# Transposes grouped by PSUM bank, one copy per group, in three places of an attention and feed-forward kernel

## What is computed

```python
def _L0_attn_ref(x, w_qkv, w_out):
    qkv = (x @ w_qkv).reshape(b, s, 3, HEADS, HEAD_DIM)
    q, k, v = (qkv[:, :, 0], qkv[:, :, 1], qkv[:, :, 2])
    scores = jnp.einsum('bqhd,bkhd->bhqk', q / sqrt(HEAD_DIM), k)
    scores = jnp.where(causal_mask[None, None], scores, NEG)
    attn = jax.nn.softmax(scores, axis=-1)
    return jnp.einsum('bhqk,bkhd->bqhd', attn, v).reshape(b, s, HIDDEN) @ w_out

def _L0_ffn_ref(x, weight, lora_A, lora_B, router_w):
    base = jnp.einsum('btd,od->bto', x, weight)
    probs = softmax(jnp.einsum('btd,ed->bte', x, router_w))
    # w_dense: the two largest, normalised, zeros elsewhere
    Ax = jnp.einsum('nd,erd->ner', x_flat, lora_A)
    expert_out = jnp.einsum('ner,ne,eor->no', Ax, w_dense, lora_B) * SCALING
    return base + expert_out.reshape(B, T, OUT_F)

x = x + _layernorm(_L0_attn_ref(_layernorm(x), w_qkv, w_out))
x = x + _layernorm(_L0_ffn_ref(_layernorm(x), weight, lora_A, lora_B, router_w))
```

## Time and profile before

| | us |
|---|---|
| median of 3 runs | 2517.46 (2517.17 to 2564.19) |
| the profiled execution | 2518.34 |
| its span on the slowest core (core 2) | 2516.8 |
| spans of the eight cores | 2499.6 to 2516.8 |

### The profile page before, as it was taken

The page is one execution under the profiler, slowest core; times in us unless marked ns, Lnnn a source line. Parts: engine busy times, 40 slices in busy tenths (PEclk is TensorE's granted clock), DMA queues, the critical chain, the costliest instruction groups (busy, mean ns, idle before and its releaser), DMA issues.

```text
span 2516.8 us, 28407 instructions; the slowest of 8 cores (2499.6 to 2516.8 us)
## 1 busy us (share of the span) xinstructions
PE 1788.2 (71%) x9387; PEld 928.9 (37%) x9552; DVE 742.5 (30%) x2497; ACT 691.8 (27%) x1393; POOL 42.1 (2%) x59
## 2 busy tenths in 40 slices
PE   1228878887887887788789788459990555666654
PEld 1114444444444444344444444224440233233332
DVE  4552122122212212221221222114442244333342
ACT  2221242143133214313322431302121233333331
POOL 0000000000000000000000000000000000000000
PEclk9998878977887897888788789679995777777777
DMA  7212011011101101110110100351218200000000
GB/s 151 101 67 26 1 26 26 4 23 26 26 1 26 26 1 26 26 25 2 26 26 1 26 1 1 55 112 67 84 67 141 43 34 34 17 34 34 34 34 34
DMA packets 48653, 95.25 MB, mean 38 GB/s; under 512 B 5248, under 2 KB 38144, under 8 KB 42368
## 3 DMA queue, kind: packets, MB, share of 16 engines
q0 software_dynamic: 46064, 76.58, 15.7%
q1 hardware_dynamic: 2448, 16.85, 2.0%
HBM read 119.67 MB, written 16.78 MB: 54 GB/s over the span
## 4 chain that ended last, share of the span: by engine, by line
PE 65%; ACT 12%; DVE 9%; issue 8%; another core or an unknown queue 4%; DVEq 0%; DMA 0%; ACTq 0%; POOL 0%; SPq 0%; POOLq 0%
PE P_qkv L303 26%; PE P_b L680 10%; PE P_qkv L453 9%; ACT expT L399 7%; PE P_e L534 4%; PE P_o L534 4%; DVE sst L151 3%; PE P_t L341 2%; ACT expT L425 2%; PE P_u L636 1%; PE P_qkv L416 1%; DVE Vaug L349 1%; ACT xln L250 1%; PE P_x L667 1%
## 5 line engine op out<-in xcount | busy, mean ns | idle before, releaser
L303 PE MATMUL P_qkv<-A,wbf 128*128 128x512 bf16 x3008 | 661.4, 380 | 20.6 <-DVE att L470 17.2
L303 PEld LDWEIGHTS P_qkv<-A,wbf 128*128 128x128 bf16 x3072 | 300.0, 98 | 377.0 <-issue 19.5
L453 PE MATMUL P_qkv<-Vaug,expT 128*128 128x129 bf16 x2176 | 258.4, 304 | 18.8 <-DVE srcp L464 15.7
L680 PE MATMUL P_b<-A,x2T 128*128 128x512 bf16 x992 | 241.3, 405 | 4.4 <-issue 3.5
L453 PEld LDWEIGHTS P_qkv<-Vaug,expT 128*128 128x128 bf16 x2176 | 223.7, 141 | 35.8 <-issue 27.6
L425 ACT ACTIVATE expT<-P_sc,cbuf 128x512 bf16<-128x512 f32 (+1 forms) x128 | 74.8, 585 | 544.3 <-PE P_t L341 542.0
L636 PE MATMUL P_u<-cbuf,xln 128*128 128x128 bf16 x256 | 54.8, 260 | 199.7 <-ACT x2T L643 180.0
L326 DVE CAST Kbf<-P_qkv 128x512 bf16<-128x512 f32 x64 | 44.3, 692 | 419.1 <-PE P_qkv L303 419.1
L680 PEld LDWEIGHTS P_b<-A,x2T 128*128 128x128 bf16 x1024 | 106.4, 105 | 135.6 <-issue 33.0
L534 PE MATMUL P_e<-wo_bf,A 128*128 128x512 bf16 x501 | 112.9, 383 | 56.2 <-DMA wo_bf<-w_out 55.6
L435 DVE TENSOR_TENSOR expT<-expT,cbuf 128x128 bf16<-128x128 bf16 x256 | 57.5, 225 | 321.4 <-ACT expT L425 314.7
(11 more groups left out here) (82 smaller groups left out, 1613.7 us busy)
## 6 DMA issues: line engine op xcount, KB each, us to landing
wbf<-wqkv POOLq DMA_DIRECT2D x16, 1536.0 KB, 14.3
expT<-x SPq DMA_DIRECT2D x16, 1024.0 KB, 6.0
xio<-x POOLq DMA_DIRECT2D x16, 1024.0 KB, 5.1
out<-ost POOLq DMA_DIRECT2D x16, 1024.0 KB, 4.6
wo_bf<-w_out POOLq DMA_DIRECT2D x2, 4096.0 KB, 41.5
A<-weightT POOLq DMA_DIRECT2D x2, 4096.0 KB, 42.2
sat<-at POOLq DMA_DIRECT2D x1, 512.0 KB, 57.2
sbf<-bflat POOLq DMA_DIRECT2D x1, 512.0 KB, 60.0
```

What stands on the lines that cost most here:

```text
L303: _q=col0, _p=wpar: e.matmul(P_qkv[:, _q:_q + 512], wbf[:, 6144 * _p + 384 * _c + 128 * _m: 6144 * _p + 384 * _c + 128 * _m + 128], A1[:, ...
L453: _q=qt: e.matmul(P_qkv[:, _a:_a + 129], expT[:, 512 * _i + 128 * _u: 512 * _i + 128 * _u + 128], Vaug[:, 129 * _i:129 * _i + 129], start= ...
L680: e.matmul(P_b[:, 512 * _f:512 * _f + 512], x2T[:, 2048 * _p + 128 * _c: 2048 * _p + 128 * _c + 128], A2[:, 2048 * _c + 512 * _f: 2048 * _ ...
```

## The change

In all three places, transposes are grouped: several go into one PSUM bank side by side, only the last one signals, and one copy with a strided access pattern takes them all. The data, the number of transposes and the banks used are the same.

- Layer norm 1: 4 groups of 4 transposes; 4 copies of 512 columns in place of 16 of 128 (destination: four runs of 128 columns, 2048 apart).
- V: 2 groups of 8; 2 copies of 1024 columns in place of 16 (destination: eight runs of 128 at a pitch of 129). The first transpose of a group waits for two blocks of VTs in place of one.
- Feed-forward: 2 groups of 8; 2 ScalarE copies of 1024 columns in place of 16; `x2T_ready` of a chunk is now its group's copy.

```diff
-                for ch in range(NCH):
-                    slot = ln1_slots[(16 * t + ch) % 8]
-                    bank = (16 * t + ch) % 8
...
+                for grp in range(4):
+                    bank = (4 * t + grp) % 8
+                    slot = ln1_slots[bank]
+                    gwb = B.gw([bank])
+                    for j in range(4):
+                        ch = 4 * grp + j
+                        B.emit("tensor", lambda e, _p=par, _c=ch, _j=j,
+                               _pt=slot: e.transpose(
+                                   _pt[:, 128 * _j:128 * _j + 128],
+                                   xln[:, 2048 * _p + 128 * _c:
+                                       2048 * _p + 128 * _c + 128], sid),
+                               waits=([(c["act"], xlv), consts_c] + gwb)
+                               if j == 0 else (),
+                               inc=(c["pe"] if j == 3 else None))
+                    tv = c["pe"].v
+                    dv = B.emit("vector", lambda e, _t=t, _g=grp, _pt=slot:
                                 e.tensor_copy(
+                                    A1[:].rearrange("p (c f) -> p c f",
+                                                    f=2048)
+                                    [:, 4 * _g:4 * _g + 4,
+                                     128 * _t:128 * _t + 128],
+                                    _pt[:, 0:512].rearrange(
+                                        "p (c f) -> p c f", f=128)),
                                 waits=[(c["pe"], tv)], inc=c["dve"])
...
-                for k in range(NCH):
-                    pt = P_t1 if k % 2 == 0 else P_t2
-                    bank = 6 + k % 2
...
+                for grp in range(2):
+                    pt = P_t1 if grp == 0 else P_t2
+                    bank = 6 + grp
+                    gwb = B.gw([bank])
+                    for j in range(8):
+                        k = 8 * grp + j
...
+                               waits=([(c["dve"],
+                                        max(vt_block[2 * grp],
+                                            vt_block[2 * grp + 1]))] + gwb
...
+                               if j == 0 else (),
+                               inc=(c["pe"] if j == 7 else None))
+                    tv = c["pe"].v
+                    av = B.emit("vector", lambda e, _g=grp, _pt=pt:
                                 e.tensor_copy(
+                                    Vaug[:].rearrange("p (k f) -> p k f",
+                                                      f=129)
+                                    [:, 8 * _g:8 * _g + 8, 0:128],
+                                    _pt[:, 0:1024].rearrange(
+                                        "p (k f) -> p k f", f=128)),
+                                waits=[(c["pe"], tv)], inc=c["dve"])
...
-                for ch in range(NCH):
-                    pt = P_u1 if ch % 2 == 0 else P_u2
-                    bank = 6 + ch % 2
...
+                for grp in range(2):
+                    pt = P_u1 if grp == 0 else P_u2
+                    bank = 6 + grp
+                    gwb = B.gw([bank])
+                    for j in range(8):
+                        ch = 8 * grp + j
...
+                               waits=([(c["act"], xl2)] + gwb) if j == 0
+                               else (), inc=(c["pe"] if j == 7 else None))
+                    tv = c["pe"].v
+                    av = B.emit("scalar", lambda e, _p=par, _g=grp, _pt=pt:
                                 e.activation(
+                                    x2T[:, 2048 * _p + 1024 * _g:
+                                        2048 * _p + 1024 * _g + 1024],
+                                    _pt[:, 0:1024], AF.Copy),
                                 waits=[(c["pe"], tv)], inc=c["act"])
                     B.sg([bank], c["act"], av)
-                    x2T_ready[ch] = av
+                    for j in range(8):
+                        x2T_ready[8 * grp + j] = av
```

More of the change, by code:

```diff
@@ L336, in build_program @@
                 vt_dve = c["dve"].v
-                for k in range(NCH):
-                    pt = P_t1 if k % 2 == 0 else P_t2
-                    bank = 6 + k % 2
[L341 to L348, removed]
-                                e.tensor_copy(
-                                    Vaug[:, 129 * _k:129 * _k + 128],
-                                    _pt[:, 0:128]), waits=wv, inc=c["dve"])
+                for grp in range(2):
[4 more added lines that the diff above has]
+                        k = 8 * grp + j
+                        B.emit("tensor", lambda e, _k=k, _j=j, _pt=pt:
+                               e.transpose(
+                                   _pt[:, 128 * _j:128 * _j + 128],
+                                   VTs[:, 128 * _k:128 * _k + 128], sid),
+                               waits=([(c["dve"],
+                                        max(vt_block[2 * grp],
+                                            vt_block[2 * grp + 1]))] + gwb
+                                      + ([(c["dve"], vaug_ones)]
+                                         if h == 0 and grp == 0 else []))
+                               if j == 0 else (),
+                               inc=(c["pe"] if j == 7 else None))
+                    tv = c["pe"].v
+                    av = B.emit("vector", lambda e, _g=grp, _pt=pt:
+                                e.tensor_copy(
+                                    Vaug[:].rearrange("p (k f) -> p k f",
[4 more added lines that the diff above has]
+                                waits=[(c["pe"], tv)], inc=c["dve"])
@@ L631, in build_program @@
                 xl2 = xl2_next
-                for ch in range(NCH):
-                    pt = P_u1 if ch % 2 == 0 else P_u2
-                    bank = 6 + ch % 2
[L635 to L642, removed]
+                for grp in range(2):
[4 more added lines that the diff above has]
+                        ch = 8 * grp + j
+                        B.emit("tensor", lambda e, _p=par, _c=ch, _j=j,
+                               _pt=pt: e.transpose(
+                                   _pt[:, 128 * _j:128 * _j + 128],
+                                   xln2[:, 2048 * _p + 128 * _c:
+                                       2048 * _p + 128 * _c + 128], sid),
+                               waits=([(c["act"], xl2)] + gwb) if j == 0
+                               else (), inc=(c["pe"] if j == 7 else None))
+                    tv = c["pe"].v
+                    av = B.emit("scalar", lambda e, _p=par, _g=grp, _pt=pt:
                                 e.activation(
-                                    x2T[:, 2048 * _p + 128 * _c:
-                                        2048 * _p + 128 * _c + 128],
-                                    _pt[:, 0:128], AF.Copy),
+                                    x2T[:, 2048 * _p + 1024 * _g:
+                                        2048 * _p + 1024 * _g + 1024],
+                                    _pt[:, 0:1024], AF.Copy),
                                 waits=[(c["pe"], tv)], inc=c["act"])
                     B.sg([bank], c["act"], av)
-                    x2T_ready[ch] = av
+                    for j in range(8):
+                        x2T_ready[8 * grp + j] = av
                 B.sg([("xln2", par)], c["pe"], c["pe"].v)
```

11 lines of the change are left out of this document (removed).

## The result

The changed kernel takes 2367.45 us (median; the kernel before, on the same chip, 2517.55), a ratio of 0.9393 with the interval 0.9378 to 0.9408: faster by 6.1%. The profiled execution took 2361.73 us, its span 2360.2 us, and 156.6 us less than the profiled execution before. Some executions of these kernels, in which the cores of a die run at a lower clock, take some per cent longer; they count in the medians given here, not in the ratios, intervals and profiles.

What follows compares the result with a forecast made beforehand. Only the heads were taken as near TensorE's limit; transpose-copy alternations lay on the chain of heads and feed-forward tiles. 2518.3 less 56 (V), 60 (x2T) and 2 (layer norm 1), clock at nothing, gave 2400 us, range 2370 to 2440.

Steps and rivals of the forecast that it cites:

- V's transposes: In each head, grouped transposes and two merged copies save 3.5 us; sixteen heads: 56 us (45 to 62).
- The spacing: Between V's grouped transposes in a head: taken as 0.09 us, with bounds 0.06 and 0.13.
- Rival 1: Strided copies run one element at a time (V: 1.21 us each); 2423 us in all; chance 0.12.
- x2T: In the feed-forward, two ScalarE copies of 1.02 us let P_b start 4.0 us sooner a tile; fifteen tiles: 60 us.
- wait for su: Feed-forward: su is ready with 5 us of room; its transpose waiting for ScalarE would prove the forecast wrong.
- Layer norm 1: Its grouped transposes and copies save 0.1 us a tile; 16 tiles: 2 us (5 gained to 4 lost).
- Clock: Granted clock's effect set to nothing; bounds 1 us either way a head, 1.3 gained to 1.7 lost a feed-forward tile.
- the middle stages: Output projection and two weight loads, between heads and feed-forward: not touched, forecast saving 0.
- Rival 3: Clock gives: V done before 768.8, first scores fast, P_b warms sooner; 36 us more, 2365 to 2385; chance 0.08.
- Rivals 2: Clock takes back 26 us in P_b and 16 in heads: 2442, up to 2467; chance 0.09, another 0.04 within 2%.
- 4: Feed-forward: P_b never gets full clock, 27.3 us a tile's 64 matmuls; 195 us lost, 2595 us in all; chance 0.02.
- 5: A hidden wait (bank guard, drains of att) holds the second group: within 2%, counted in a chance of 0.04.

Runs made afterwards that it cites:

- pad19: The changed kernel with one VectorE memset of 1024 columns behind V's copies in each head, holding up the scores; 2357.3 us in one profiled execution.
- pad37: The changed kernel with two VectorE memsets (4096 and 192 columns) behind V's copies in each head, holding up the scores; 2428.4 us, ratio 0.9635.
- ffn_only: The kernel before with only the feed-forward's x2T transposes grouped; 2452.0 us, ratio 0.9779.
- v_only: The kernel before with only V's transposes grouped; 2437.1 us, ratio 0.9664.
- ffn_early: The changed kernel with the next tile's x2T transposes and copies planned ahead of this tile's layer norm 3; 2302.8 us, ratio 0.915.
- best: ffn_early plus vwait, with the next tile's layer norm 2 moved behind the router and su in the queues; 2214.6 us, ratio 0.8788.
- small: The changed kernel with V and x2T transposes still grouped, but sixteen copies of 128 columns back to back; 2387.2 us, ratio 0.9483.
- pad11: The changed kernel with one VectorE memset of 64 columns behind V's copies in each head; 2384.0 us in one profiled execution.
- vwait: The changed kernel with score matmuls waiting for V's last cast instead of the last copy into Vaug; 2328.4 us, ratio 0.9247.

## Why the prediction was off

**V's transposes: right.** 3.5 us a head forecast, 3.7 measured (59 us for 56). The spacing was taken as 0.09 us and was (0.61 - 0.22) / 7 = 0.056, the other bound. The merged copy cost 0.689 us for 0.69. Rival 1, one element at a time (1.21 us), is refuted. The Trainium skill's page "VectorE: DVE Perf Modes", section "Mode 2×_1P — pack two bf16 into one 32-bit read", asks for a 4-byte aligned start; half of this copy's eight runs begin on 2-byte addresses, and all 32 copies took 683 to 696 ns. The measurement decides against that rule for this case.

**x2T: right.** From the tile's layer norm 3 statistics to its P_b it was 15.39 us before (2088.00 to 2103.39) and is 11.36 after (1984.44 to 1995.80): 4.03 us for 4.0, 60.5 us in all. The copies took 1.014 us for 1.02, so bf16 and f32 do lie on one line on ScalarE. TensorE did not wait for su.

**Layer norm 1: at the good end of its bounds.** In its timeline the sixteen transposes now stand in 1.86 us, (1.86 - 0.31) / 15 = 0.103 us apart:

```profile
104.94 1.86 PE L263 MATMUL P_qkv<-cbuf,xln 128*128 128x128 bf16 x16 [8.85 <-ACT xln L250]
105.64 1.71 DVE L272 COPY A<-P_qkv 128x512 bf16<-128x512 bf16 x4 [3.19 <-PE P_qkv L263]
107.26 2.46 DVE L151 BATCH_NORM_STATS2 sst<-expT 128x6 f32<-128x512 f32 x4
```

The forecast had named 0.107 for transposes without a semaphore each, 0.2 us a tile, and took 0.1, 2 us in all, with 5 us as the bound. The tile period is 10.82 us for 11.06, 0.24 a tile and 4 us in all. The stage ended 4.8 us earlier, 0.7 of that because its first load came 0.7 us sooner.

**Clock: this is the step that failed,** a term of the sum set to nothing. "I leave it at nothing, with bounds of ... 1 us either way a head." The heads gained 1.2 us each from it, 19 us, outside the bound; the feed-forward about 0.5 us a tile, 8 us, inside it. The direct terms were right, and the miss is one of size. With the 3 us of V, 3 of layer norm 1 and 5 of the middle stages these are the difference to 2361.7. Rival 3 is what happened (2365 to 2385 at a chance of 0.08), but not for the reason given there. "V is done before 768.8, where it fell" would make any earlier V better; yet `pad19`, later than the changed kernel, has the faster rest, and so has `pad37`, later than the kernel before. The prediction had given 0.09 to the clock taking something back and 0.08 to its giving something, so it did not see which way the term would go. The range then left out rival 3's low end by choice, and the result lies 3 us below it. What in the profile of before spoke for a wider bound was there: the earlier trace rows show the clock falling inside the head, and its price could have been read as both levels of the part after it, from all full to all half, rather than 1 us. In the nine kernels of the table it moved 2.9 us.

**Rivals 2, 4 and 5** did not occur. P_b's 64 matmuls took 14.2 to 15.8 us, not 27.3. What the Trainium skill's page "TensorE: Matmul & The Clock Gate", section "Part 4: PE-mode transpose", says of transposes and the clock, no run here separates.

**Not settled.** By what rule the granted clock falls and rises where it does. The runs show that the time at which the scores begin moves it, and that what TensorE did in the stretch made no difference to the mean; they also show heads of one program with the same stretch that differ by 3 to 4 us, so something besides the stretch has a part, and what it is stays open. Whether the feed-forward's 0.5 us a tile is the same effect was not tested. It is argued from its cycle of three, which `ffn_only` has too, and from P_b's 64 matmuls, 15.1 us in the mean for 15.3 in `v_only`, which are 0.2 of the 0.5. The 4.7 us of the middle stages were not tested either; the two load stops in other runs, 44.8 to 57.5 us, vary by more.

## To carry to other kernels

When two engines take turns over two banks with a short operation each, it is the turn that costs (0.35 us a piece here against 0.137 back to back); group by bank first, the larger copy is the smaller part. Where the granted clock changes inside a loop body, a saving or a delay does not add up: give the clock a range of its own, with both levels as its ends, keep it in the forecast's range, and compare by the period of the loop and by the part of it that nobody edited, on all cores. And look in the list of waits at what is longest, not only at what is most frequent: moving the 15 waits of 9.8 us that this change left in place took 3.9 us off a tile in `ffn_early`, as much as the 112 that it removed, and opened the way to 3.5 more in `best`.

## What was unexpected in the hardware

- Waiting can pay: 1.1 us added to each head of the kernel before took it from 2515.9 to 2500.3 us, 1.26 us added to each head of the changed one left it no slower (2357 for 2362).
- The pattern repeats over heads: all equal (before, `small`), in pairs (after, the first eight), in threes (`pad37` 87.63, 88.40, 86.94, the first nine), though the work of every head is the same. Runs of equal heads stand at 88.7 us (before), 85.3 (`small`) and 81.9 (`pad11` on core 7, `vwait` on core 7 too), the last with stretches as different as 2.92 and 1.55 us.
- VectorE's bf16 copies out of PSUM lie on one line, whether the destination is one run, four or eight: 226 ns for 128 columns, 425 for 512, 689 for 1024, so 0.52 ns an element from each to the next, half the f32 price of the earlier trace rows.
- A memset's own row is not its price. Those of 64, 1024, 3120 and 4096 bf16 columns took 0.11, 0.91, 2.66 and 3.47 us by their rows, 0.83 ns for each further column; the idle time before them grew with their length (0.35, 0.79 and 0.99 us for the last three), and the stretch, 2.92, 3.92 and 6.10 us with the first three, grew by 1.04 ns a column.
